# A graph network on one core: the loops of the ranking stage and of the edge passes written out, counts and addresses as constants

## What is computed

```python
def attention(h, src, dst, extra):                  # layers 0 and 2
    z = h @ W
    score = leaky_relu((z * a_l).sum(-1)[src] + (z * a_r).sum(-1)[dst] + extra, 0.2)
    w = exp(score - segment_max(score, dst)[dst])
    return segment_sum(w * z[src], dst) / segment_sum(w, dst)

def relational(h, src, dst, etype):                 # layer 0, three times, with attention
    return segment_sum(h[src] @ W_rel[etype], dst) + h @ W_loop

def gated(h, src, dst):                             # layer 1
    gate = sigmoid(relu(concat(h[src], h[dst]) @ We1) @ We2 + be2)
    return segment_sum(gate * h[src], dst)

def transformer_conv(x, src, dst, e):               # layer 3, twice
    alpha = (q(x)[dst] * (k(x)[src] + e)).sum(-1) / sqrt(C)
    w = exp(alpha - segment_max(alpha, dst)[dst])
    return segment_sum(w * (v(x)[src] + e), dst) / segment_sum(w, dst)
# e = concat(msg, cos(rel_t * Wt + bt)) @ We, rel_t = last_update[src] - t
```

## Time and profile before

| | |
|---|---|
| median of 3 runs | 13423.76 us (13402.09 to 13431.12) |
| span of the profiled execution | 13400.0 us (its own time is not listed) |
| instructions executed | 212567 |
| busy: VectorE | 10400.3 us, 78% |
| busy: TensorE, products | 8527.8 us, 64% |
| busy: GpSimd | 6926.8 us, 52% |
| busy: ScalarE | 3614.6 us, 27% |
| DMA of instructions, q8 and q14 | 51 and 83 packets |

### The profile page before, as it was taken

One profiled execution on the slowest core, in us unless ns is written; L12 is line 12 of the kernel. 1 busy time (PEld: TensorE's weight loads), 2 busy tenths in 40 slices (PEclk: granted clock), 3 DMA queues, 4 the chain that ended last, 5 costly groups with the idle time before them and its releaser, 6 DMA issues. The chain is left out here.

```text
span 13400.0 us, 212567 instructions
## 1 busy us (share of the span) xinstructions
PE 8527.8 (64%) x52858; PEld 6962.8 (52%) x52859; DVE 10400.3 (78%) x15015; ACT 3614.6 (27%) x7819; POOL 6926.8 (52%) x7047
## 2 busy tenths in 40 slices
PE   4663477776777677775465652777266666567764
PEld 3553245554455535654455542555266666566664
DVE  8666569974799748996688875888778888688888
ACT  0111133332333233332244431333211111111111
POOL 2775047750477407772277750777145555255553
PEclk8555688877888788887688875666588888788887
DMA  4334754444544474443255550222233334233333
GB/s 182 113 113 119 244 206 106 106 80 193 192 106 106 72 292 123 106 106 53 79 145 145 146 111 19 55 55 54 19 103 106 107 107 105 75 108 105 105 106 72
DMA packets 720185, 1523.62 MB, mean 114 GB/s; under 512 B 364796, under 2 KB 416585, under 8 KB 680627
## 3 DMA queue, kind: packets, MB, share of 16 engines
q0 software_dynamic: 306624, 795.04, 25.0%
q1 hardware_dynamic: 413427, 727.07, 15.9%
HBM read 1050.48 MB, written 471.10 MB: 114 GB/s over the span
## 5 line engine op out<-in xcount | busy, mean ns | idle before, releaser
L970 POOL DMA_INDIRECT h<-table,edges_ring x3984 | 3856.5, 968 | 1889.0 <-issue 1154.3
L1147 PE MATMUL bank<-h,edges_onehot 128*128 128x260 f32 (+1 forms) x7968 | 1986.6, 406 | 652.3 <-issue 469.0
L1147 PEld LDWEIGHTS bank<-h,edges_onehot 128*128 128x128 f32 x7968 | 1570.6, 246 | 978.1 <-issue 717.4
L970 POOL DMA_INDIRECT edges_rows<-table,edges_ring x1512 | 1527.0, 1010 | 716.0 <-issue 431.0
L1122 PE MATMUL bank<-ident,edges_score 128*4 128x128 f32 x5280 | 1027.7, 360 | 1021.5 <-DVE edges_score L1288 737.9
L1258 DVE TENSOR_TENSOR_SCAN bank<-edges_fresh,edges_top,bank 4x1024 f32<-4x1024 bf16 x660 | 1541.5, 2336 | 144.9 <-PE bank L1122 141.2
L1265 DVE TENSOR_TENSOR_SCAN edges_top<-edges_fresh,bank 4x1024 f32<-4x1024 bf16 x660 | 1493.8, 2263 | 0.6 <-issue 0.3
L1122 PEld LDWEIGHTS bank<-ident,edges_score 128*4 128x4 f32 x5280 | 497.6, 104 | 1339.0 <-DVE edges_score L1288 784.9
L1314 DVE TENSOR_TENSOR acc<-acc,bank 128x260 f32 (+1 forms) x2640 | 908.9, 344 | 164.4 <-PE bank L1147 60.4
L2017 POOL DMA_INDIRECT rec<-dst,slots x782 | 797.0, 1019 | 432.7 <-issue 432.4
L1203 ACT ACTIVATE edges_onehotT<-bank 128x1024 bf16<-128x1024 bf16 (+1 forms) x550 | 562.1, 1022 | 1153.3 <-PE bank L1087 715.9
(11 more groups left out here) (346 smaller groups left out, 18152.3 us busy)
## 6 DMA issues: line engine op xcount, KB each, us to landing
table<-x SPq DMA_DIRECT2D x154, 1040.0 KB, 7.9
edge_score<-edge_feat SPq DMA_DIRECT2D x220, 512.0 KB, 3.8
table<-h SPq DMA_DIRECT2D x77, 1040.0 KB, 7.9
table<-source_typed_rows SPq DMA_DIRECT2D x63, 1040.0 KB, 8.1
h<-table,edges_ring POOLq DMA_INDIRECT x3984
edge_feat<-edge_score SPq DMA_DIRECT2D x110, 512.0 KB, 2.9
dst_row<-dst_rows SPq DMA_DIRECT2D x71, 704.0 KB, 4.2
buf<-rec SPq DMA_DIRECT2D x44, 840.0 KB, 5.2
```

The costliest lines, as they stand in the source:

```text
L970: pool.indirect_dma_start(out=rows[s % R][:, j, :], out_offset=None, in_=table, in_offset=bass.IndirectOffsetOnAxis(ap=ring[:, s * ST + j: ...
L1147: ins = pe.matmul(sum_b[k % 3], onehot[s][:, j, :], rows[s][:, j, A0:W], start=j == k * GT, stop=j == (k + 1) * GT - 1)
```

## The change

The loops of `superblocks` and `superblock_pairs` are written out on every engine that calls them, as are GpSimd's loop over turns, SyncE's loops of loads and stores, and the loop over pairs of chunks in the ranking stage, on all engines. Each superblock then has its own instructions; the values that waits compare with, and the addresses that came from the loop's register, are constants. The bins' numbers are still loaded into registers. The loops of the counting, folding, table and closing stages stay. The whole diff (line numbers of what follows move by 2 to 6):

```diff
--- before.py
+++ after.py
@@ -895,9 +895,7 @@
         step((q + n // RING, n % RING), (q + m // RING, m % RING), (q, s))
     step((0, 0), None, None)
     step((0, 1), (0, 0), None)
-    for s in range(RING):
-        full(0, s)
-    with engine.Fori(1, (NSUPER - 2) // RING) as q:
+    for q in range((NSUPER - 2) // RING):
         for s in range(RING):
             full(q, s)
     end = (NSUPER - 2) // RING
@@ -911,7 +909,7 @@
     for s in range(RING):
         step(after((0, s)), (0, s))
     full = (NSUPER - 1) // RING
-    with engine.Fori(1, full) as q:
+    for q in range(1, full):
         for s in range(RING):
             step(after((q, s)), (q, s))
     for s in range(NSUPER - 1 - RING * full):
@@ -972,7 +970,7 @@
                                     ).then_inc(gathered[s % R], 16)
     for s in range(TURN):
         one(0, s)
-    with pool.Fori(1, NSUPER // TURN) as q:
+    for q in range(1, NSUPER // TURN):
         for s in range(TURN):
             one(q, s)
     for s in range(NSUPER % TURN):
@@ -1062,9 +1060,7 @@
                     park(sp)
                     sp.dma_start(fresh[s][:, :], g.fresh_d[bass.ds(u * SLOTS_SB, SLOTS_SB + 1)].partition_broadcast(HEADS)
                                  ).then_inc(fresh_in[s], 16)
-                load(0, 0)
-                load(0, 1)
-                with sp.Fori(1, NSUPER // 2) as q:
+                for q in range(NSUPER // 2):
                     load(q, 0)
                     load(q, 1)
 
@@ -1431,7 +1427,7 @@
                 load(0, 0)
                 load(0, 1)
                 store(0, 0)
-                with sp.Fori(0, NSUPER // 2 - 1) as q:
+                for q in range(NSUPER // 2 - 1):
                     load(q + 1, 0)
                     store(q, 1)
                     load(q + 1, 1)
@@ -1892,9 +1888,7 @@
 
             def chunk_pairs(engine, fn):
 
-                fn(0, 0, 0, CH, CH)
-                fn(1, 0, 1, CH, CH)
-                with engine.Fori(1, NCH // 2) as q:
+                for q in range(NCH // 2):
                     fn(q * 2, q, 0, CH, CH)
                     fn(q * 2 + 1, q, 1, CH, CH)
                 fn(NCH - 1, NCH // 2, 0, CH, TILES - FULL)
```

## The result

The change makes the kernel **slower**, by 0.4%: 13478.2 us in the median of 5 runs (13463.7 to 13485.0) against 13409.8 (13402.1 to 13431.1) for the kernel before, ratio 1.0042 with a 95% interval of [1.0028, 1.0055]. The prediction said 13317.

The account below looks back on a forecast made before the run. POOL was taken to bound four edge passes and ranking; in the gated and conv passes it had slack. Gated -65 and conv -42 gave -107 us, from 13424 to 13317; own range 13285 to 13350, 8 in 10 from 13205 to 13420.

Parts of the forecast that it names:

- Gated pass, -65: Gated pass: superblocks fall from 12.65 to 12.0 us, some 45 us from table load, 20 from registers; bounds -45 to -68.
- The sample of 12.02 us: Gated pass: an already written-out superblock of the kernel before took 12.02 us, taken as what the change makes everywhere.
- the held load: Gated pass, ScalarE: sine's table load held behind the wait for VectorE's angle once in four superblocks; some 45 us to gain.
- POOL is no new bound: 0.946 + 0.31 us times 8 is 10.1 us: Gated pass: GpSimd's eight gathers and gaps need 10.1 us a superblock, so they don't limit the forecast 12.0.
- Conv passes, -42: Two conv passes: register additions and bin loads saved, 0.2 us in each of 2 x 104 superblocks, -42 us.
- Slower: the clock: Rival, conv passes: TensorE idles longer, more products run at 1.2 GHz; +65 + 34 - 65 = +34, 13458 us; chance 0.08.
- the filling of a pipeline: Conv passes: argument against the slow written-out samples, that these eight superblocks are the first of their pass.
- Ranking, 0: Ranking stage: POOL's scatters and gaps fill its whole 1035 us, so no change was forecast.
- a possible gain only: Ranking stage: 57 us open if scatters fell to a gather's 0.946 us; none of it taken.
- The POOL-bound passes, 0: Three layer 0 passes and layer 2's: POOL's instructions and gaps stay the same, about 1111 us each as before.
- The code's size, 0: Whole kernel: streams grow from some 18,000 to 133,000 instructions, but fetching is hidden; price 0.
- rival by the rule of the Trainium skill on taken branches: Gated and conv passes: the change removes page fetches at jumps back, 78 us more gain, 13239 us; chance 0.04.
- both slower cases: Whole kernel: lower TensorE clock in conv, 13458 us, chance 0.08; fetching holds TensorE, 13527 us, chance 0.05.

Follow-up runs that it names:

- e3_one_kept: The change with three loops kept (ScalarE's in gated pass, VectorE's in ranking, TensorE's in conv passes): ranking 1041.5, gated 1337.3, conv 1629.8 and 1644.7 us.
- e5_bins_half: The change plus one TensorE load (conv 1), four products (conv 2), two VectorE copies (ranking), VectorE's gated loop kept: 1639.9, 1628.5, 1037.8, 1335.4 us.

## Why the prediction was wrong

- *Gated pass, -65.* Right in what it rests on, and a little low: 11.88 us a superblock where 12.0 was forecast, -76, which is past the forecast's own bound of -68. The sample of 12.02 us was one of the two lengths that alternate, the longer. Of the parts, ScalarE's (the held load, with its own registers) is 50 us alone and 23 with the others written out (forecast 45), VectorE's registers 21 (forecast 20), TensorE's 5. One step was wrong without harm to the number: "POOL is no new bound: 0.946 + 0.31 us times 8 is 10.1 us" took the gather of another pass. By the earlier trace rows it is 908/100 + 8 x 0.31 = 11.6 us, just below where the pass ended.
- *Conv passes, -42.* This is the step that failed: "I take the register work at the gated pass's price, 0.2 us". The size is about right where the granted clock is high: with the filler, at 0.94 to 0.96, looped and straight code differ by 17 and 18 us a pass, 0.17 a superblock. Without it, the clock falls from 0.85 and 0.83 to 0.78 when TensorE is written out, its same products take 1133 us instead of 1079, and the two passes lose 91 us where 42 were to be gained. The rival "Slower: the clock" had the mechanism (TensorE does wait longer ahead of these products, 127.3 us instead of 106.2) and nearly the sum (+65 + 34; measured +52.2 and +38.8), and it got 0.08. Its evidence was in the earlier trace rows: the only written-out conv superblocks that existed took 15.63 and 15.45 us at 0.77 and 0.80. I set them aside as the filling of a pipeline, and took instead the price of a pass in which TensorE isn't waited for in the same way. In the gated pass I had believed the sample; in the conv passes I explained it away.
- *Ranking, 0.* The second step that failed: the stage is POOL's, "with no wait in which a faster VectorE or TensorE could be felt". The gaps stayed (0.305 us), the scatters didn't, 1.077 us on average instead of 1.019: how long a scatter takes depends on what VectorE runs when it starts, and that cost 45 us. The earlier trace rows had the hint, scatters of 1.019 us beside gathers of 0.946, and I read it as a possible gain only. No rival had it.
- *The POOL-bound passes, 0.* 2.2 to 2.9 us each, within the 10 allowed, and not shown to come from the change.
- *The code's size, 0.* Right: 915 packets of instructions where there were 134, and no loss that follows them. The prediction's rival by the rule of the Trainium skill on taken branches ("Runtime: NRT & Kernel Launch", section "Instruction fetch mechanics") expected a gain on top. The rule speaks of branches to pages that aren't resident; the earlier trace rows show no fetch in the loop, and no stage of these runs shows the gain.
- *The numbers.* The sign rested on the conv passes, two thirds of the work outside POOL's pace, and both signs were open by the rows. 0.11 for slower was far too little, and the range for 8 in 10 ended at 13420, below the 13424 that it was counted from: it left both slower cases out.

Open: why TensorE's clock is lower in this order of products. The runs show that it follows where products come, that products put into its waits raise it (0.78 to 0.86 with eight, 0.95 with twelve in all), and that time follows it for the most part (but the first conv pass took 1629.8 us at 0.86 in e3_one_kept and 1639.9 at 0.88 in e5_bins_half); they don't show the rule. Open too is the chip of 15164 us.

## What to carry to other kernels

Taking instructions away on one engine moves its work against the others', and that can cost more than the instructions did: price the new meeting points (what runs on VectorE when a GpSimd transfer starts, where TensorE's gaps fall), not the saving alone. Where part of a loop is written out already, that part is a measurement of the change; if it isn't faster, believe it. Where TensorE has gaps and its granted clock is well below 1 in a stage that waits for it, try products of no use in the gaps before anything else: here they gave 1.2% with the loops left alone, on one chip; on the one of 15164 us the same kernel came out 1.3% slower than the kernel before, in one run of each. So try it on the chip that counts.

## What the runs showed of the hardware

- **A scatter of GpSimd waits for some of VectorE's operations.** If it starts while L1751 runs, it takes 0.83 us plus what is left of that operation (medians): with 1.45 us left it takes 2.29 (after), with 0.65 left 1.48 (e5_bins_half), with 0.45 left 1.28 (before). One that starts 0.06 us ahead of it takes 0.96. From 300 to 1200 us of the kernel before, 62 scatters began under L1751 and took 1.28 us on average, 62 under the reduction L1981 and 62 under L1999, which reads PSUM, and took 0.96. The same holds for gathers in the first conv pass: in the loop's 104 superblocks, 94 that began under the one-hot L946 took 1.56 on average, 164 under L1250 0.94. The row of short operations L1977 is less simple: of 155 scatters that began under one of them between 300 and 1200 us, 124 took about 1.0 us, as that one operation asks, and 31 took 1.53: these began when 0.70 us of the whole row of eleven were left, and took 0.83 us plus that. The Trainium skill, "SBUF — State Buffer", section on the two separate sides, says that VectorE and GpSimd share a pair of ports, that the one which starts first holds it for its whole instruction, and that VectorE takes it also with an operation that has two inputs in SBUF, if GpSimd's operation reads SBUF. The trace agrees: L1751, L946 and L1977 have two inputs there, the others one, and a scatter that starts just ahead of L1751 isn't held.
- **Who comes first decides, and the phase locks.** VectorE starts when a scatter lands, so much the same distance repeats in most chunks: some 0.2 us of it are worth 45 us of a stage of 1034 here (0.07 us behind a scatter's start before, 0.15 ahead of one after).
- **Filler products raised the granted clock and paid, on the chips where the kernel before takes 13400 us.** 0.78 to 0.95, 1689 to 1550 us in the first conv pass, though TensorE makes 16% more products (8860 in 103 superblocks, 7624 without). Register loads in the same places left it at 0.78 and 1690 us. On the chip of 15164 us the looped kernel with them had 0.91 and 1761 us.
